# Graph attention over 8192 keys: ten blocks of a row turned by DMA, adjacency loads issued by ScalarE

## What is computed

```
def reference(x, adj, ks):                    # x 8192x128, adj 8192x8192 int32, ks 8192x128
    h = relu(layernorm(x))                    # over the last axis, eps 1e-5, no weights
    scores = h @ ks.T                         # 8192 x 8192
    scores = leaky_relu(scores, 0.2)
    scores = where(adj > 0, scores, -9e15)
    attn = softmax(scores, axis=1)
    return x + attn @ ks
```

## Time and profile before

| | |
|---|---|
| three runs | 1599.86 us median (1594.65 to 1601.03) |
| the profiled execution | 1600.33 us, span 1598.5 us from first to last instruction |
| granted TensorE clock | 0.998 of full speed over the span |
| PE busy | 1563.9 us |
| DVE, ACT, POOL busy | 1421.2, 1344.5, 1335.2 us |
| adjacency loads | 512 of 512 KB |
| turned blocks | 572 |

### The profile page before, as it was taken

How to read it: one execution, slowest core, us unless ns; L and a number is a source line. 1 busy time by engine, 2 the same in 40 slices (tenths; PEclk the granted TensorE clock), 3 DMA queues, 4 the chain that set the end, 5 groups by cost and what they waited for, 6 DMA issues and landing times.

```text
span 1598.5 us, 37557 instructions
## 1 busy us (share of the span) xinstructions
PE 1563.9 (98%) x13202; PEld 1156.3 (72%) x13202; DVE 1421.2 (89%) x2532; ACT 1344.5 (84%) x2002; POOL 1335.2 (84%) x1350
## 2 busy tenths in 40 slices
PE   5799999999999999999999999999999999999998
PEld 3477777777777777777777777777777777777777
DVE  6899888988889898998998998998899899899897
ACT  7688888888888888888888888888888888888885
POOL 3788888888888888888888888888888888888885
PEclk9999999999999999999999999999999999999999
DMA  8999999999999999999999999999999999999995
GB/s 282 283 273 271 277 270 273 294 261 280 278 278 273 274 280 290 287 265 293 287 270 289 268 289 279 273 271 285 282 258 308 274 272 291 270 276 279 266 281 102
DMA packets 700602, 437.67 MB, mean 274 GB/s; under 512 B 629760, under 2 KB 629760, under 8 KB 700416
## 3 DMA queue, kind: packets, MB, share of 16 engines
q1 hardware_dynamic: 700416, 435.27, 112.5%
HBM read 276.82 MB, written 4.19 MB: 176 GB/s over the span
## 4 chain that ended last, share of the span: by engine, by line
PE 86%; DMA 4%; ACT 3%; DVE 2%; POOL 2%; issue 2%; SPq 0%; DVEq 0%; POOLq 0%; ACTq 0%
PE ps_out L428 25%; PE ps_out L429 13%; PE ps_scores L401 12%; PE ps_scores L403 12%; PE ps_scores L402 12%; PE ps_T L412 11%; DMA keys_in<-keys_in 4%; ACT scores L501 1%; DVE scores L621 1%; POOL keys_in L337 1%; DVE mask L603 1%; POOL keys_in L339 1%; ACT scores L480 1%; ACT scores L492 1%; PE ps_out L379 0%
## 5 line engine op out<-in xcount | busy, mean ns | idle before, releaser
L339 POOL TENSOR_TENSOR keys_in<-scores,keys_in 128x512 f16<-128x512 f32 x572 | 719.2, 1257 | 46.2
L621 DVE CUSTOM_DVE_ANT_0 scores<-ps_scores,mask,minus_scale 128x1024 f32<-128x1024 f32 x512 | 654.0, 1277 | 16.8 <-PE ps_scores L403 2.2
L492 ACT ACTIVATE scores<-scores 128x1024 f32<-128x1024 f32 x512 | 537.6, 1050 | 77.6 <-DVE pair_min L621 77.6
L337 POOL CAST keys_in<-scores 128x512 f16<-128x512 f32 x572 | 460.2, 804 | 159.3 <-ACT scores L501 155.2
L501 ACT ACTIVATE scores<-scores,neg_max 128x1024 f32<-128x1024 f32 x512 | 583.1, 1139 | 0.1
L428 PE MATMUL ps_out<-keys,keys_in 128*128 128x256 f16 x2225 | 428.7, 273 | 5.2 <-DMA keys_in<-keys_in 4.8
L636 DVE TENSOR_TENSOR probsT_lo<-ps_T,probsT_hi 128x512 f16<-128x512 f32 x452 | 311.2, 689 | 125.1 <-ACT probsT_hi L509 116.6
L401 PE MATMUL ps_scores<-keysT_hi,hT_hi 128*128 128x512 f16 x1024 | 389.0, 380 | 13.6 <-DVE keysT_lo L592 8.4
L429 PE MATMUL ps_out<-keys,keys_in 128*128 128x128 f16 x2225 | 398.0, 219 | 0.0
L509 ACT ACTIVATE probsT_hi<-ps_T 128x512 f16<-128x512 f32 x441 | 260.7, 591 | 153.9 <-PE ps_T L412 150.1
L402 PE MATMUL ps_scores<-keysT_lo,hT_hi 128*128 128x512 f16 x1024 | 389.1, 380 | 0.0
(11 more groups left out here) (57 smaller groups left out, 845.5 us busy)
## 6 DMA issues: line engine op xcount, KB each, us to landing
adj_in<-in_adj_dram SPq DMA_DIRECT2D x512, 512.0 KB, 5.3
keys_in<-keys_in SPq DMA_TRANSPOSE x572, 5.5
x_in<-in_x_dram SPq DMA_DIRECT2D x16, 256.0 KB, 4.4
keys_in<-in_L_gnn_ks_dram SPq DMA_DIRECT2D x8, 512.0 KB, 7.2
out_dram<-out_tile SPq DMA_DIRECT2D x16, 256.0 KB, 3.8
keys<-keysT_hi SPq DMA_TRANSPOSE x8, 5.3
keys<-keysT_lo SPq DMA_TRANSPOSE x8, 4.8
```

The costliest lines, as they stand in the source:

```text
L337: nc.gpsimd.tensor_copy(half[:, 0:BLOCK], probs(t, b)).then_inc(half_hi_ready, 1)
L339: nc.gpsimd.tensor_tensor(half[:, BLOCK:2 * BLOCK], probs(t, b), half[:, 0:BLOCK], ALU.subtract) \
L492: nc.scalar.activation(s, s, ACT.Prelu, alpha=1.0 / SLOPE).then_inc(leaky_ready, 1)
L621: nc.vector.tensor_tensor_reduce(out=score_pair(q, p), in0=ps_scores[:, slots, :].rearrange("p s k -> p (s k)"), in1=mask[:, (p // 2) % 2, ...
```

## The change

Three things. Block 4 joins the blocks that go the DMA way, in all tiles but the last: ten of sixteen. The adjacency loads move from SP's list to ACT's: one load of 2048 columns (1 MB) fills a whole buffer; three of them are issued between ACT's copies of the keys at the start, and from then on one at the end of sub-steps 3, 7, 11 and 15, three buffers ahead. The number of buffers stays four, with one semaphore each. SP keeps the turned blocks, the keys, x and the output.

```diff
--- before.py
+++ after.py
@@ -40,7 +40,7 @@
     TURN_LAG = 5
     ADD_LAG = 10
 
-    BY_DMA = tuple(b for b in range(BLOCKS) if b % 2 == 1 or b in (12,))
+    BY_DMA = tuple(b for b in range(BLOCKS) if b % 2 == 1 or b in (4, 12))
     BY_PE = tuple(b for b in range(BLOCKS) if b not in BY_DMA)
     LAST_BY_DMA = (1, 3, 5, 7, 9)
 
@@ -116,7 +116,7 @@
         ps_out = psum("ps_out", [P, 2, BLOCK], fp32)
 
 
-        adj_loaded = [sem(f"adj_loaded{s}") for s in range(2 * ADJ_SLOTS)]
+        adj_loaded = [sem(f"adj_loaded{s}") for s in range(ADJ_SLOTS)]
         keys_loaded = [sem(f"keys_loaded{p}") for p in range(PAIRS)]
         x_loaded = [sem(f"x_loaded{s}") for s in range(2)]
         stored = sem("stored")
@@ -243,13 +243,6 @@
                 sp.wait_ge(out_ready, (g + 1) * GROUP)
                 sp.dma_start(out_groups[g], out_tile[:, g % 2, :, :]).then_inc(stored, 16)
 
-            def load_adj(q, p):
-                n = q * PAIRS + p
-                if n >= 2 * ADJ_SLOTS:
-                    sp.wait_ge(mask_ready, n // 2 - ADJ_SLOTS + 1)
-                sp.dma_start(adj_in[:, n // 2 % ADJ_SLOTS, n % 2 * PAIR:(n % 2 + 1) * PAIR],
-                             adj_tiles[q // GROUP, q % GROUP, :, p * PAIR:(p + 1) * PAIR]).then_inc(adj_loaded[n % (2 * ADJ_SLOTS)], 16)
-
             def turn(t, b):
                 n = nth_dma(t, b)
                 sp.wait_ge(half_lo_ready, n + 1)
@@ -271,16 +264,11 @@
             for p in range(PAIRS):
                 c = slice(p * PER_PAIR, (p + 1) * PER_PAIR)
                 sp.dma_start(keys_in[:, c, :], key_pairs[p]).then_inc(keys_loaded[p], 16)
-            for p in range(6):
-                load_adj(0, p)
             load_x(1)
 
             def step(i, odd, more, this, prev, ahead):
                 for j in range(BLOCKS):
                     if j % 2 == 1:
-                        q, p = divmod((i + 1) * PAIRS + j // 2 + 6, PAIRS)
-                        if q < TILES:
-                            load_adj(q, p)
                         if i == -1:
                             turn_keys(j // 2, HI)
                             if j // 2 < 4:
@@ -341,8 +329,7 @@
 
             def make_first_mask(k):
 
-                pool.wait_ge(adj_loaded[2 * k], 16)
-                pool.wait_ge(adj_loaded[2 * k + 1], 16)
+                pool.wait_ge(adj_loaded[k], 16)
                 pool.wait_ge(mask_ready, k)
                 if k >= 2:
                     pool.wait_ge(masked_ready, 2 * k - 2)
@@ -474,6 +461,13 @@
 
         @block.scalar
         def _(act):
+            def load_adj(q, k):
+                n = q * LOADS + k
+                if n >= ADJ_SLOTS:
+                    act.wait_ge(mask_ready, n - ADJ_SLOTS + 1)
+                act.dma_start(adj_in[:, n % ADJ_SLOTS, :], adj_tiles[q // GROUP, q % GROUP, :, k * LOAD:(k + 1) * LOAD]) \
+                    .then_inc(adj_loaded[n % ADJ_SLOTS], 16)
+
             def copy_keysT(b):
                 act.wait_ge(keysT_done, b + 1)
                 dst = keysT[:, pair_cols(b // 2)].rearrange("d (q c) -> d c q", c=PER_PAIR)
@@ -511,6 +505,8 @@
 
             for b in range(BLOCKS):
                 copy_keysT(b)
+                if b in (3, 5, 7):
+                    load_adj(0, (b - 3) // 2)
             act.wait_ge(scale_steps, SCALED)
             split_keysT_hi(0)
             split_keysT_hi(1)
@@ -531,6 +527,10 @@
                     split = behind(i, j, T_LAG, by_pe, this, prev)
                     if split and split[0] < TILES - 1:
                         split_probs_hi(*split)
+                    if j % 4 == 3:
+                        q, k = divmod((i + 1) * LOADS + j // 4 + 3, LOADS)
+                        if q < TILES:
+                            load_adj(q, k)
 
             steps(step)
 
@@ -596,8 +596,7 @@
             def make_mask(q, k):
 
                 n = q * LOADS + k
-                dve.wait_ge(adj_loaded[2 * (n % ADJ_SLOTS)], (n // ADJ_SLOTS + 1) * 16)
-                dve.wait_ge(adj_loaded[2 * (n % ADJ_SLOTS) + 1], (n // ADJ_SLOTS + 1) * 16)
+                dve.wait_ge(adj_loaded[n % ADJ_SLOTS], (n // ADJ_SLOTS + 1) * 16)
                 if q > 0 or k >= 2:
                     dve.wait_ge(masked_ready, q * PAIRS + 2 * k - 2)
                 nc.vector.tensor_scalar(mask[:, k % 2, :], adj_in[:, n % ADJ_SLOTS, :], 0, MASKED, ALU.is_le, ALU.mult) \
```

## The result

The changed kernel takes 1864.59 us in the median of four runs (1800.88 to 1938.49), the kernel before beside it 1597.92 (1594.65 to 1601.03): a ratio of 1.133, 95% interval 1.129 to 1.137. So the change is 13% slower by the ratio and 17% by the medians; the forecast was 1587, its range 1572 to 1635. The profiled execution is the fastest of the four, 1800.88 us with a span of 1799.1.

What follows compares the result with a forecast made beforehand. PE, busy 98% at 24.10 us a tile, bounds the kernel; with block 4 moved, POOL binds at 23.9. Gain 0.20 us x 63 = 12.6, all else counted as nothing: 1600.33 to 1587.7, by the median 1587; range 1572 to 1635.

Steps and rivals of the forecast that it cites:

- the one on the loads: Adjacency loads: 0.26 MB more a tile, 291 GB/s over 23.9 us, against slices up to 308; counted as nothing.
- the transfers become the bound: Rival, DMA transfers: if 278 GB/s is the most, a tile's 6.96 MB take 25.0 us, 1657 in all; chance 0.13.
- 9 x 1.70 + 8 x 0.57 = 19.9 us: SP's issuing per tile before the change, from median turns and loads; falls to 17.0, counted as nothing on the sum.
- Loads of 1 MB instead of two of 512 KB: Adjacency loads: same bytes, half as many landings, each issued over 10 us ahead of its mask; counted as nothing.
- Loads move to ACT: SP loses 512 load issues, ACT gets 256, of about 0.57 us, fitting under the leaky instruction's 0.94; counted as nothing.
- ACT becomes the bound: Rival: load issues on ACT wait for SP's turn issues, 1.2 us each; ACT needs 24.8 us, 1644 in all; chance 0.19.
- PE minus 0.44 us: Block 4's four transposes leave PE in 63 tiles; PE alone would then need 23.66 us a tile instead of 24.10.
- POOL at 23.9, bounds 23.70 to 24.15: Block 4's split comes to POOL, which becomes the engine with the longest tile; gain 0.20 us a tile, 12.6 us.
- POOL swallows all of it: Rival: POOL, slowed by DVE's masks, needs 24.15 us a tile; no change, 1597 to 1606; chance 0.16.
- PE stays the bound: Rival: POOL needs 23.70 and PE 23.66 us a tile; 1574, at the very best 1572.6; chance 0.12.
- POOL still waits over 1 us a tile: Sign in the changed profile that the forecast is wrong and another engine binds; POOL's wait was expected under 30 us.
- The cover for block 7's turn: Block 7: 10.3 us from subtraction's end to PE's use; less 1.85, the median 5.5 us turn fits, some 3 spare.

Runs made afterwards that it cites:

- part 6: Ten blocks turned, one queue, 512 KB loads issued in pairs after every fourth block, against ten blocks with single loads (1695.88 us): 1734.59 us.

## Why the prediction was wrong, step by step

- *The step that failed* is the one on the loads: "over 23.9 us that is 291 GB/s, and single slices of the run already show up to 308. Counted as nothing." A slice of 40 us at 308 GB/s is no proof of what a mix can hold. With nothing else in their way loads alone reach 403 GB/s, nine turns with eight loads 288, ten turns with eight loads 271, and ten with four loads of 1 MB 257 on one queue and 219 on two. In the kernel before the transfers already needed 22.7 to 23.5 of 24.1 us; those of the changed kernel need 26.6 on one queue and 31.1 on two, where the forecast allowed 23.9. The rival "the transfers become the bound" had the mechanism, and its 25.0 us a tile (1657) was nearest to the 25.7 (1696) of the tenth turn alone; but its 278 GB/s is a ceiling of this mix only, and it had no cost for the size of the loads or for the second queue.
- *The same error in the rows of SyncE.* I took 9 x 1.70 + 8 x 0.57 = 19.9 us as issuing work. The minimum, 1231 ns, is the work; the rest of the median 1702 comes with the loads and is, as I read it, waiting for room. The nearly full queue stood in that row and was read as work that could go.
- *"Loads of 1 MB instead of two of 512 KB ... the same bytes"*, counted as nothing: 97 us on one queue. Alone, the size makes no difference (10.1 and 10.4 us a tile); between turns, 26.6 against 25.1. Two loads of 512 KB at the same places of SyncE's list already cost 39 of the 97 (part 6). Why the larger load mixes worse is open.
- *"Loads move to ACT"*, counted as nothing on the sum: right for ACT, whose issue is 0.33 us flat with the next exponential still 0.94 to 0.97 us behind the leaky instruction; wrong for the transfers, 72 us by the medians, 19 by the runs that the ratio counts, and 81 at the least with nine blocks. The rival "ACT becomes the bound" falls. The Trainium skill, Perfetto Trace Analysis, DMA Instruction — HWDGE (DVE, Sync), has one issuer at a time lock the block that makes descriptors; no such wait shows in ACT's 256 issues (334 to 389 ns), beside turns whose issue takes up to 9149 ns.
- *PE minus 0.44 us*: nearly right. A good tile has 23.82 us of PE, where 23.66 was forecast.
- *POOL at 23.9, bounds 23.70 to 24.15*: nearly right, as the run without loads shows, but at its upper end, 24.2. The gain of 12.6 us would have been none even without transfers (1597.6). The rival "POOL swallows all of it" describes that run; the one run at 1569.9 would fit the rival "PE stays the bound" (1572.6 at the very best), but it left no trace.
- *"POOL still waits over 1 us a tile"* was named as the sign of another engine; it waits 165.1 + 92.0 us, 4 a tile, and the other "engine" is the transfers. The sign "landings of turns beyond 8 us" came too (21.4).
- *The cover for block 7's turn*, 10.3 us against landings of 5.5 to 8.1: the wait ahead of the issue was missing in it.

Open: why a turn and several loads of another queue hold each other up. From 503 to 505 us of the long tile the packets go in steps of some 320 ns: in each, one load packet (8 KB, 309 to 318 ns) and one 256-byte packet of a turn that lasts 18 ns, while 15 to 20 more of the turns' packets stay under way for 315 to 670 ns. It looks as if one DMA engine alternated between the two queues and the turn moved at its pace; but the records name no engine, and they do not explain the loads' packets that are held for 2 to 4 us elsewhere in that tile. That plain copies do not suffer fits, but no run separates the pace of the engines from other causes. The Trainium skill, DMA: Bandwidth & Descriptors, Queues, rings and completion order, has each engine serve its queues in turn, packet by packet; the steps would fit that, and are no proof of it. Its section Issuing engines are not separate DMA queues says a second issuer only saves issue time; here, transfers alone, the second queue cost 4.5 to 9.8 us a tile beside turns. Open too is why pairs cost more and the eighth load less than the sum says.

## What to carry to other kernels

Before transfers are added, compute how full the queue is in time, not in GB/s: the transfers alone in a kernel without computation, or the issuing engine's idle time between issues, and take an issue that lasts longer than its minimum as a sign that it waits for room. Loads on a second queue beside DMA transposes are to be tried with one load under way at a time, and measured; leaving both on one queue, single loads of 512 or 256 KB alternating with nine turns, was the best found here (1598 and 1596 us). Where two engines lengthen each other's instructions, as the casts and the masks do here, take the upper bound for both when one of them becomes full.

## What was not expected of the hardware

- Ten blocks alone on SyncE's queue took as long turned (13.9 us) as plainly copied (14.0). But both are the pace of the issues, 1.33 us for a turn and two of 0.65 for a copied block, with landings that hardly vary; neither shows what the transfer itself costs:

```profile
L79 SPq DMA_TRANSPOSE turned<-halves x146: 1231/1334/1367, 3498.9 to 3698.8; - x146
...
DMA to landing us min/median/max: 3.3/3.4/3.7
```

```profile
L82 SPq DMA_DIRECT2D turned<-halves x290: 594/647/654, 2939.4 to 3139.8; - x145
...
DMA to landing us min/median/max: 2.3/2.3/2.5
```

- The Trainium skill, Advanced Engine Details and Errata, X-Bar Transpose (TRN2), says that transposing transfers are as fast as regular ones. On one queue with eight loads of 512 KB that nearly holds here (22.8 us with nine turns, 21.6 with copies); beside 1 MB loads of another queue it does not (33.6 against 21.1).
- Mixed on one queue, loads and turns take longer than their own distances add up to. Loads alone landed every 1.30 us (10.4 us for eight), and in the kernel with only the tenth block a turn behind a turn landed 0.98 us after it (mean of 300 to 1400 us); by an estimate from these two, eight loads and ten turns would need 20.2 us, and alone they took 25.1. In that kernel a load landed 1.74 us behind a turn.
